# Softmax division of two PSUM banks: one reciprocal for the pair, in place of one reciprocal per bank

## The reference

```python
q, k, v = jnp.split(x @ w_qkv, 3, axis=-1)          # then to heads, rotary on q and k
attn = jax.nn.softmax(jnp.einsum('bhid,bhjd->bhij', q, k) * scale, axis=-1)
out = jnp.einsum('bhij,bhjd->bhid', attn, v)
out = out.transpose(0, 2, 1, 3).reshape(B, n, INNER)
return out @ w_out + b_out
```

## Time and profile before

| | |
|---|---|
| median of three runs | 675.54 us (675.03 to 677.36) |
| profiled execution, first to last instruction (span) | 672.1 us |
| own time of the profiled execution outside the span | not listed; the median stands 3.4 us above the span |
| PE busy | 547.4 us (81%) |
| PE weight loads busy | 431.2 us (64%) |
| DVE busy | 454.7 us (68%) |
| ACT busy | 306.2 us (46%) |
| POOL busy | 248.8 us (37%) |
| TensorE clock granted, mean | 0.919 of full |

### The profile page before, as it was taken

How to read it: one execution, slowest core, us unless ns; L and a number is a source line. 1 busy time by engine, 2 the same in 40 slices (tenths; PEclk the granted TensorE clock), 3 DMA queues, 4 the chain that set the end, 5 groups by cost and what they waited for, 6 DMA issues and landing times.

```text
span 672.1 us, 21383 instructions
## 1 busy us (share of the span) xinstructions
PE 547.4 (81%) x8984; PEld 431.2 (64%) x8984; DVE 454.7 (68%) x1336; ACT 306.2 (46%) x507; POOL 248.8 (37%) x197
## 2 busy tenths in 40 slices
PE   0888898897888877978988788789887735999992
PEld 0575576566746755666567466646765635999991
DVE  5577665957877578488675776977569676444444
ACT  1454834266457332844754347457435313343330
POOL 6403600432145032502620415145014173777652
PEclk9979979889899897999999979999899585999997
DMA  5000007600000000000001000000000013151314
GB/s 134 1 2 1 2 3 222 248 2 5 14 2 2 25 10 3 2 18 1 3 3 33 2 3 3 17 1 3 3 1 3 2 50 109 46 149 53 106 38 140
DMA packets 17425, 24.71 MB, mean 37 GB/s; under 512 B 2578, under 2 KB 12180, under 8 KB 17268
## 3 DMA queue, kind: packets, MB, share of 16 engines
q1 hardware_dynamic: 14836, 18.17, 8.8%
q0 software_dynamic: 2496, 5.18, 2.3%
HBM read 17.12 MB, written 9.33 MB: 39 GB/s over the span
## 4 chain that ended last, share of the span: by engine, by line
PE 63%; DVE 17%; ACT 10%; issue 6%; POOL 2%; DMA 1%; DVEq 0%; SPq 0%; ACTq 0%
PE turn L677 8%; PE small L815 8%; PE score L785 7%; PE score L745 7%; PE score L905 6%; PE small L917 6%; PE small L726 4%; PE turn L694 4%; PE turn L755 4%; PE turn L757 3%; PE small L852 3%; ACT probT L625 3%; ACT xnT L588 2%; DVE stats L939 2%; DVE prob L1074 2%
## 5 line engine op out<-in xcount | busy, mean ns | idle before, releaser
L498 POOL TENSOR_TENSOR rstd<-veps,mhalf 128x8 f32<-128x8 f32 x28 | 46.4, 1657 | 247.7 <-DVE veps L979 247.7
L625 ACT ACTIVATE probT<-turn 128x512 f32<-128x512 f32 x96 | 53.1, 595 | 92.5 <-PE turn L677 92.3
L1072 DVE TENSOR_REDUCE top<-score 128x16 f32<-128x1024 f32 (+1 forms) x48 | 58.6, 1220 | 43.8 <-PE score L785 43.8
L785 PE MATMUL score<-kE,qT 32*32 32x64 f32 (+1 forms) x3072 | 56.9, 258 | 16.7 <-issue 10.5
L785 PEld LDWEIGHTS score<-kE,qT 32*32 32x32 f32 (+1 forms) x3072 | 47.8, 121 | 30.9 <-issue 28.1
L677 PE MATMUL turn<-ident,prob 128*128 128x128 f32 x384 | 59.5, 305 | 2.7 <-ACT prob L619 2.4
L1074 DVE TENSOR_TENSOR prob<-score,top 128x1024 f32<-128x1024 f32 x48 | 58.8, 1225 | 1.6
L619 ACT ACTIVATE prob<-prob 128x1024 f32<-128x1024 f32 x48 | 50.1, 1057 | 10.0 <-DVE prob L1074 9.8
L548 POOL DMA_INDIRECT answers<-y_sb,home x46 | 44.9, 976 | 23.8 <-DVE y_sb L1208 16.4
L612 ACT ACTIVATE kE<-turn,hmask 128x512 f32<-128x512 f32 x64 | 39.9, 686 | 28.9 <-PE turn L757 28.6
L815 PE MATMUL small<-v_s,probT 128*64 128x34 f32 x1024 | 42.4, 240 | 11.7 <-ACT probT L625 6.2
(11 more groups left out here) (126 smaller groups left out, 1059.1 us busy)
## 6 DMA issues: line engine op xcount, KB each, us to landing
w_all<-in_w SPq DMA_DIRECT2D x2, 2048.0 KB, 20.4
dispatched<-in_slots_init SPq DMA_DIRECT2D x2, 1518.0 KB, 10.2
slots<-dispatched SPq DMA_DIRECT2D x6, 396.0 KB, 4.7
pairs<-answers SPq DMA_DIRECT2D x8, 256.0 KB, 3.7
ws<-in_w_s SPq DMA_DIRECT2D x4, 257.0 KB, 2.7
wt<-in_w_t SPq DMA_DIRECT2D x4, 257.0 KB, 2.6
x_in<-in_x SPq DMA_DIRECT2D x2, 512.0 KB, 4.4
vec<-in_vec_in SPq DMA_DIRECT2D x4, 256.0 KB, 4.0
```

The lines of the kernel that those rows point to most:

```text
L498: nc.gpsimd.tensor_tensor(rstd[:, q.nth % 4, :], veps[:, q.nth % 4, :], mhalf[:, :], ALU.pow).then_inc(rstd_ready, 1)
L625: nc.scalar.activation(probT[:, q.nth % 2, 2 * k:2 * k + 2, 2 * h:2 * h + 2, :].rearrange("p k g n -> p k (g n)"), turn[:, u % 2, :].rearr ...
L785: last = nc.tensor.matmul(score[b * n:(b + 1) * n, g, c * 2 * n:(c + 1) * 2 * n], qT[rows, tok:tok + n], kE[rows, :, tok:tok + n], start=q ...
L1072: nc.vector.tensor_reduce(tops, mine, AX_X, ALU.max).then_inc(top_ready, 1)
```

## The change

In `divide`, DVE now waits for both banks of the pair, makes one reciprocal of the 2 x 16 sums, waits for it, and then makes the two products, one for each bank, in the same order as before. A product releases its bank as before. Nothing else is changed.

```diff
                     first = mix.smalls + (0 if q.kind == S else 2 * q.group)
+                    dve.wait_ge(small_full, first + 2)
+                    src = small[:, :, 0:16 * VW].rearrange("p b (h d) -> p b h d", d=VW)
+                    nc.vector.reciprocal(den[:, :, :], src[:, :, :, DH]).then_inc(den_ready, 1)
+                    dve.wait_ge(den_ready, q.nth + 1)
                     for z in range(2):
                         u = first + z
-                        dve.wait_ge(small_full, u + 1)
-                        src = small[:, u % 2, 0:16 * VW].rearrange("p (h d) -> p h d", d=VW)
-                        nc.vector.reciprocal(den[:, u % 2, :], src[:, :, DH]).then_inc(den_ready, 1)
-                        dve.wait_ge(den_ready, 2 * q.nth + z + 1)
                         nc.vector.tensor_tensor(o_nrm[:, q.group * 2 + z, :].rearrange("p (h d) -> p h d", d=DH),
-                                                src[:, :, 0:DH], den[:, u % 2, :, None].broadcast_to([P, 16, DH]),
+                                                src[:, u % 2, :, 0:DH], den[:, u % 2, :, None].broadcast_to([P, 16, DH]),
                                                 ALU.mult).then_inc(small_free[u % 2], 1)
```

## The result

The changed kernel is **slower by 0.39%** (ratio of the times 1.0039, 95% interval 1.0021 to 1.0056): 678.97 us against 676.48 us, medians of 20 runs each. By the ratio that is 2.6 us, between 1.4 and 3.8. (The ratio is taken over all runs and isn't the quotient of the two medians, which are 2.5 us apart.) The forecast was 3.9 us. All 20 runs of the changed kernel last 1.8 to 1.9 us longer than their span, so the 3.4 us that the prediction put around the profiled span of before was only partly time outside the span: the profiled execution of before, 672.1 + 1.9 = 674.0 us, was itself 2.5 us shorter than the median of 676.48.

The account below looks back on a forecast made before the run. PE, busy 81% of the span, was taken as the bound, with DVE mostly early at the divisions. Terms 2.5 + 0.1 + 0.17 + 1.14 + 0 = 3.9 us, added to 675.54, gave 679.4 us; range 676.0 to 683.5.

Parts of the forecast that it names:

- DVE early or late decides, not DVE's load: At the divisions: DVE idled before a reciprocal in 24 places, so a shorter division that starts later is no gain.
- The reciprocal of 128x32 at 350 ns: Merged reciprocal on DVE: 350 ns, from 6.1 ns per further column; bounds 252 and 504 ns.
- Temporal mixes, 0.36 us each, seven times: First pair of seven temporal mixes: bank 0 comes free 0.36 us later and PE waits exactly that; 2.5 us.
- Spatial pairs with a glow, 0.21 each: Second spatial group, four places: product ends 0.30 us later, glow covers 0.09, 0.21 is new; 0.84 us.
- Half 0 of layers 1 to 3, sum 0: Spatial groups there: about +0.11 in layer 1, +0.1 in layer 2, -0.2 us in layer 3; sum 0.
- Last output step, +0.17: Second pair of the last temporal mix, before `out`: 0.38 us later, 0.21 covered by a glow, 0.17 us new.
- The eighth mix: Layer 3, half 1, first temporal pair: DVE is late, so only the longer reciprocal counts; 0.10 us.
- The sum, 3.9 us: Whole kernel: delays at all places together make it 3.9 us slower, 679.4 us.
- DVE is the bound: Rival, at the divisions: each of 32 pairs 0.19 us shorter, 6.1 us faster, 669.4 us; chance 0.05.
- One reciprocal costs as much as two: Rival, at the merged reciprocal: the change removes nothing, 682.2 us; chance 0.08.
- The delays are taken up again: Rival, in PE's later "issue" pieces: delays vanish at half the places, leaving 2 us, 677.5 us; chance 0.18.
- The clock: Rival, on PE: one more 1.2 GHz stretch costs 1.7 us, 681.1 (chance 0.14); one fewer, 677.7 (chance 0.05).

Follow-up runs that it names:

- wait_both: Kernel before, but DVE waits for both banks of a pair, then reciprocal, product, reciprocal, product as before: 685.65 us, ratio 1.0137.
- late_only: Kernel before, reciprocal merged only in half 0's second spatial pair of layers 1 and 2 and both of layer 3: 675.52 us, ratio 1.0003.
- lend_merge: Kernel before, units 2 and 3 of a temporal mix in two idle score banks, with one reciprocal for these two: 672.67 us, ratio 0.9953.
- t_only: Kernel before, with one reciprocal for both banks in the 16 temporal pairs only: 678.41 us, ratio 1.0028.
- s_only: Kernel before, with one reciprocal for both banks in the 16 spatial pairs only: 679.29 us, ratio 1.0027.
- twice: Changed kernel, with its merged reciprocal done twice, one after the other: 689.94 us, ratio 1.0217 to the kernel before.
- lend_split: Kernel before, units 2 and 3 of a temporal mix in two idle score banks, still a reciprocal per bank: 671.28 us, ratio 0.9934.

## Why the prediction was right, point by point

- **DVE early or late decides, not DVE's load**: held, and this is what made the prediction right. 5.0 us less work on DVE and a slower kernel; wait_both shows that the wait alone costs more than the whole change, and late_only and lend_merge show the merged reciprocal gaining 0.19 us where DVE is late.
- **The reciprocal of 128x32 at 350 ns**: 356. The slope from the two rows, 6.1 ns for a column, was good: from 252 to 356 it is 6.5. Of the two statements of the Trainium skill, "VectorE: DVE Perf Modes", the one on the fixed cost with one element a cycle gave 269 ns and falls; the iterative divide ("First, the fixed hardware budget") with an estimated 385 ns is nearer, and still above the trace.
- **Temporal mixes, 0.36 us each, seven times**: the pause in front of unit 2 grew by 0.34, as said, but the cost was mis-sized. A mix takes PE only 0.20 us more (2.70 to 2.90), 1.4 in place of 2.5 for seven. The sum asked whether bank 1 would be free in time after the change, and did not ask whether it had been before: there PE waited a second time, 0.13, and the merged reciprocal takes that wait away. The stretch around the mix confirms it: from transposes to transposes of `o_nrm` 18.30, 18.33, 18.33 and 18.33 us before, in layers 0 to 3, and 18.52, 18.53, 18.54 and 18.52 after.
- **Spatial pairs with a glow, 0.21 each**: mis-sized. Measured 0.29 here, and 0.49 in wait_both where 0.40 was expected. What failed is "0.09 is covered": the modelled end of the glow was taken for the time until which PE was busy. The transposes start before that end and 0.10 behind the release, before and after. Over four places this is 0.3 us of the sum. The fifth place, without a glow, was right: PE's wait of 1.00 us became 1.29.
- **Half 0 of layers 1 to 3, sum 0**: the pair is 0.19 shorter there as computed (late_only), and the first pair's later start is passed on. From the second spatial mix to the transposes it was 2.67, 2.68 and 2.67 us in layers 1 to 3 and is 2.94, 3.44 and 2.46: +0.8 in sum, in place of 0. But t_only, which leaves the spatial pairs alone, has 3.83 in layer 2, and s_only, which merges them, 2.46; so the rest depends on the execution, and a single one does not settle it.
- **Last output step, +0.17**: mis-sized. The transposes start 2.73 us behind the start of the last 64 matmul records (546.13 - 543.40), where it was 2.26 (542.42 - 540.16): +0.47. Here too the cover of 0.21 by the end of the glow was not there. The eighth mix itself, forecast at +0.10, had a pause of 1.06 in place of 1.23: DVE came less late to it. Taken together, from the start of the eighth mix to the transposes it was 4.21 and is 4.52 us: +0.31, where the two forecasts add up to 0.27.
- **The sum, 3.9 us**: the profiled pair gives 3.9 at the same clock (0.919 both), and the 20 runs 2.6 (1.4 to 3.8). With the measured sizes it is 7 x 0.20 + 5 x 0.29 + 0.31 = 3.2 us, and 4.0 with the 0.8 that this one execution lost at half 0 of layers 1 to 3. So the excess of the forecast over the 2.6 is mostly the temporal term, 1.1 too large; the spatial term, 0.3 too small, hid a part of it. The direction and the mechanism were right. The forecast time of 679.4 is only 0.4 above the measured 678.97, and that is partly luck: the difference was 1.3 too large, and the three runs of before that it was added to lay 0.9 below the later median. The 3.9 of the profiled pair is luck too, since on its way the distance between the two executions moves up and down by more than 1 us: it is 0.82 us at the second temporal mix (159.84 - 159.02), 2.60 at the third (243.10 - 240.50) and 1.91 at the fourth (290.56 - 288.65), where the places between them add 0.8 at most and then 0.2.
- **The rivals.** "DVE is the bound" is out by the result's sign, though twice had a total that would fit it. "One reciprocal costs as much as two" is out by 356 ns. "The delays are taken up again": the change's 2.6 against 3.2 to 4.0 at the places and lend_split's 4.5 against about 7 speak for a part of it, wait_both and twice, well above their places, against it: not shown. "The clock" made no difference between the two profiled executions (109 us at 1.2 GHz in both; the changed one has one short stretch fewer, and others that are longer), but a part of the spread between executions of one kernel goes with it.

The profile of the change alone would not have been enough to say this. Among the ten profiled executions, two (s_only and late_only) are 6.5 to 7.2 us longer than that of before with code that over 12 runs moves the time by 1.8 us or less; the places in the timeline, and PE's waits by line, were the parts that repeated.

## What to carry to other kernels

Before two short operations on one engine are merged to save their fixed cost, ask whether that engine is early or late at that place: a merged operation starts when the last of its inputs is there and frees the first buffer later, and where the engine was early this cost the producer more here than the merge saved. Here 0.19 us was saved per pair, against 0.24 to 0.49 us of a later start. Read the price from the start of the producer's step to its next one, and not from its first pause: in the temporal mix the first pause grew by 0.34 us and the second one shrank, and the price was 0.20. If the producer waits for the consumer in the middle of its own work, another buffer is worth more than a faster consumer: two idle PSUM banks gave 4.5 us, where the merge lost 2.6.

## What the runs showed of the hardware that was not expected

The times of one kernel spread more than its changes. The 20 runs of the changed kernel went from 675.68 us (span 673.8, mean clock 0.921) to 684.16 us (span 682.3, clock 0.915), and the granted clock between 0.915 and 0.930. The order of the times follows the clock only in part: 677.8 and 682.3 us of span both come at 0.915, and over the 154 runs an additional us at 1.2 GHz goes with 0.18 us of span, not with 0.5. Whether it matters where in the work the slow stretches fall is a question that no run here answers.

The cost of DVE's reciprocal is 203 ns for 8 columns, 252 for 16 and 356 for 32, about 6 to 6.5 ns for each column beyond a fixed part of some 150 ns, while the product of 256 columns takes 425 ns in all. Of the 356 ns more than half (32 x 6.5 = 208) grows with the columns and is paid merged or not. That is why merging two of them saves only 0.15 us of busy time.
